# Opening of a decoder-layer kernel: context rows scaled by Pool in the preparation, both input blocks in PSUM, one ring bank beside the scans, merged norm statistics

## What is computed

```python
x = layernorm(x + mamba(x))                 # state of 512 channels x 16, scanned over 512 steps
x = layernorm(x + cross_attention(ctx, x))  # 16 heads of 64; keys and values from 1601 + 512 rows
x = layernorm(x + experts(x))               # 8 experts, 2 chosen, 2 shared

# in mamba, for each channel d and state n
h = exp(dt * A) * h + dt * B * xs           # over time
y = sum_n(h * C) + xs * D                   # then y * silu(z) @ W_out
# in cross_attention
xn = layer_norm(ctx, g1, b1); ln = layer_norm(x, g2, b2)
q = ln @ Wq; k, v = concat([xn, ln]) @ Wkv; softmax(q k / 8) v @ Wout
```

## Time and profile before

| | us |
|---|---|
| median of 3 runs | 3148.29 (3147.78 to 3148.49) |
| the profiled execution | 3144.86 |
| its span | 3143.1 |
| preparation | 0 to 151.05 |
| scans and gate | 151.05 to 289.70 |
| bridge | 289.70 to 342.23 |
| attention and experts | 342.23 to 3143.1 |

### The profile page before, as it was taken

How to read it: one execution, slowest core, us unless ns; L and a number is a source line. 1 busy time by engine, 2 the same in 40 slices (tenths; PEclk the granted TensorE clock), 3 DMA queues, 4 the chain that set the end, 5 groups by cost and what they waited for, 6 DMA issues and landing times. The chain is left out here.

```text
span 3143.1 us, 33934 instructions
## 1 busy us (share of the span) xinstructions
PE 2954.3 (94%) x11590; PEld 1850.7 (59%) x11590; DVE 1973.0 (63%) x3403; ACT 1343.6 (43%) x2309; POOL 1070.3 (34%) x838
## 2 busy tenths in 40 slices
PE   7576899999999999999999999999999999899996
PEld 3233566656665656565656566666656565676666
DVE  5897677775658777666777776665555554452225
ACT  4642454454455454536454544354343434211121
POOL 3196466662006676600376664000000000102213
PEclk9788899999999999999999999999999999899998
DMA  5341221121121111211221212101010100411112
GB/s 218 150 163 68 74 71 58 34 65 55 38 68 58 35 58 35 71 35 38 75 58 35 71 50 63 38 15 40 19 38 15 38 15 14 168 57 53 51 44 69
DMA packets 71679, 189.84 MB, mean 60 GB/s; under 512 B 8420, under 2 KB 39272, under 8 KB 63448
## 3 DMA queue, kind: packets, MB, share of 16 engines
q1 hardware_dynamic: 67096, 172.08, 18.0%
q0 software_dynamic: 3984, 15.60, 1.5%
q10 hardware_dynamic: 432, 0.01, 0.0%
HBM read 124.59 MB, written 28.44 MB: 49 GB/s over the span
## 5 line engine op out<-in xcount | busy, mean ns | idle before, releaser
L987 ACT ACTIVATE a_carry<-a_st 128x512 f32<-128x512 f32 (+1 forms) x1088 | 649.1, 597 | 1126.7 <-PE a_st L1368 1118.7
L1380 PE MATMUL a_o<-a_carry,a_vals 128*65 128x512 f32 (+1 forms) x2176 | 1113.7, 593 | 0.0
L1145 DVE TENSOR_REDUCE a_maxes<-a_mx 128x1 f32<-128x512 f32 x1024 | 683.0, 686 | 220.0 <-PE a_mx L1296 213.3
L1368 PE MATMUL a_st<-a_q,a_kone 65*128 65x512 f32 (+1 forms) x1088 | 431.5, 397 | 0.0
L884 POOL TENSOR_TENSOR a_shared<-a_shared,a_bc 128x512 f32<-128x512 f32 x192 | 251.5, 1310 | 384.9 <-DVE a_shared L1083 384.9
L1380 PEld LDWEIGHTS a_o<-a_carry,a_vals 128*65 128x65 f32 (+1 forms) x2176 | 284.1, 137 | 103.5 <-issue 1.8
L1367 PE MATMUL a_st<-a_q,a_keven 128*128 128x512 f32 (+1 forms) x544 | 325.9, 599 | 0.7 <-issue 0.7
L855 POOL TENSOR_TENSOR a_erstd<-a_emv,a_half 128x4 f32<-128x4 f32 x8 | 8.1, 1014 | 906.9 <-DVE a_emv L1171 906.9
L1367 PE MATMUL a_st<-a_q,a_kodd 128*128 128x512 f32 (+1 forms) x544 | 314.9, 579 | 0.0
L1296 PE MATMUL a_mx<-a_kodd,a_q 128*128 128x512 f32 x512 | 298.4, 599 | 7.2 <-DVE a_maxes L1145 6.1
L1083 DVE TENSOR_TENSOR_SCAN a_shared<-a_shared 128x512 f32<-128x512 f32 x192 | 288.6, 1505 | 12.7 <-POOL a_shared L873 11.6
(11 more groups left out here) (251 smaller groups left out, 4404.9 us busy)
## 6 DMA issues: line engine op xcount, KB each, us to landing
a_bc<-m_kept_bc SPq DMA_DIRECT2D x48, 512.0 KB, 3.7
a_wt<-a_w_split SPq DMA_DIRECT2D x15, 1536.0 KB, 9.5
a_kone<-a_keven SPq DMA_DIRECT2D x32, 528.5 KB, 4.5
a_kone<-a_kodd SPq DMA_DIRECT2D x32, 528.5 KB, 4.2
e_wall<-in_w_t_dram SPq DMA_DIRECT2D x27, 512.0 KB, 9.6
a_early<-m_kept_bc SPq DMA_DIRECT2D x16, 512.0 KB, 3.7
a_w_split<-a_wt POOLq DMA_DIRECT2D x4, 1536.0 KB, 5.5
a_shared<-in_ctx_dram SPq DMA_DIRECT2D x4, 1536.0 KB
```

What stands on the lines that cost most here:

```text
L987: nc.scalar.activation(p_of(s % 4)[0:r], st[0:r, s % 2], ACT.Exp, scale=SCALE).then_inc(exp_done, 1)
L1145: nc.vector.reduce_max(maxes[:, c, t:t + 1], mx[:, i % 2], AX_X).then_inc(mx_max, 1)
L1368: nc.tensor.matmul(st[0:r, s % 2], k_one[g % 2][0:DH + 1, kt * P:kt * P + r], qm[of(g)][0:DH + 1, :], start=False, stop=True).then_inc(st_ ...
L1380: nc.tensor.matmul(ps_o[0:DH + 1, g % 2], vals[0:r, kt * HG + j, :], p_of(s % 4)[0:r], start=(kt == 0), stop=(kt == KT - 1)).then_inc(pv_d ...
```

## The change

- **Preparation.** The context statistics move to the first tap of the last batch's convolution, their sums to behind `clip_dt` of the batch before. Pool then scales all 13 context tiles (`tensor_scalar`) in the preparation. The B and C rows of states 0 and 1 are fetched there (`fetched`), and ScalarE ends with a one-column exponential.
- **Scans.** dt*xs of both channel blocks of a pair is copied to PSUM (`dtu_bank`, two banks), and VectorE makes 40 of the 64 inputs (`BY_DVE`), Pool 24. The third decay buffer takes a ring bank, so the context items share ring bank 0. Context blocks stay in that bank: ScalarE applies the gammas in place, the high part is a step of its own ("h"), the low part reads PSUM. ScalarE copies the values. xs*D enters the sums by a matmul, and `gate_first` only multiplies.
- **Bridge.** Per tile of 128 rows: statistics, then one power for both norms ("g": the second norm's factor follows from the same variance), and one scaling for the attention input ("n"); the first norm's scaling ("j") moves beside head 0. The queries are made per block ("q"). Row scores of head 0 use four banks and start before keys 3 and 4. Rows of ones and of `wo` are set by Pool ("1").

```diff
+            for t in range(CTX_T):
+                r = CL if t == CTX_T - 1 else P
+                nc.gpsimd.tensor_scalar(rows[0:r, t], rows[0:r, t], mv[0:r, t, 0:1], rstd[0:r, t:t + 1], ALU.subtract, ALU.mult)
...
+            nc.scalar.activation(cb[:, 0:1], cb[:, 0:1], ACT.Exp)
...
+                    if j == 0 and i == B - 1:
+                        context_stats(c)
...
-                if i == B:
+                if i == B - 1:
                     context_sums()
...
+                if b == B - 1:
+                    sp.wait_ge(bc_kept, 32 * B)
+                    for n, (place_of, loaded) in enumerate(fetched):
+                        sp.dma_start(place_of.rearrange("p i s -> p (i s)"), kept_bc[b, n].partition_broadcast(P)
+                                     ).then_inc(loaded, 16)
...
+BY_DVE = [u for u in range(NU) if u % 2 == 0 or u % 8 == 3]
...
+    room = {"T": 13, "V": 10, "K": 13}
+    at, all_room = 0, sum(room[what[0]] for what in early)
+    for what in early:
+        step = at * (NU - 2) // all_room
+        at += room[what[0]]
+        later = {"PE": 0, "ACT": 1 if what[0] == "T" else 2, "DVE": 3}[engine]
+        steps[step + later].append(what)
+        if what[0] == "T":
+            steps[step + later + (engine == "ACT")].append(("h",) + what[1:])
+            steps[step + later].append(("U",) + what[1:])
...
-        decay_first, dtu_bank = [mx[:, 0], mx[:, 1], ps_o[:, 1]], ps_o[:, 0]
+        decay_first, dtu_bank = [mx[:, 0], mx[:, 1], ring[:, 1]], [ps_o[:, 0], ps_o[:, 1]]
...
+            def mx_bank(g, i):
+
+                return (st if g == 0 and i % 4 >= 2 else mx)[:, i % 2]
...
             copy_keys(0)
+            sp.wait_ge(ones_set, 2)
+            load_wo(0)
...
+                if c < N_CTX:
+                    made = turned_first(what)
+                    for k in range(KD):
+                        a = nc.scalar.activation(made[:, k], made[:, k], ACT.Identity, bias=gb[:, 1, k:k + 1], scale=gb[:, 0, k:k + 1])
...
+                step(nc.vector.bn_stats(end_stats[:, t], x1_rows(b, t)))
+                step(nc.vector.bn_aggr(end_mv[:, t], end_stats[:, t]))
+                nc.vector.tensor_scalar(both_var[:, t, 0:1], end_mv[:, t, 1:2], EPS, None, ALU.add)
+                nc.vector.tensor_scalar(both_var[:, t, 1:2], end_mv[:, t, 1:2], 1.0 + EPS, EPS * EPS, ALU.mult,
+                                        ALU.add).then_inc(var_ready, 1)
...
-                    s = nc.vector.tensor_tensor(y[:, c], sums(c), y[:, c], ALU.add)
-                s.then_inc(sums_out, 1)
-                dve.wait_ge(sums_out, q + 1)
-                for c in (2 * q, 2 * q + 1):
-                    nc.vector.tensor_tensor(y[:, c], y[:, c], gate[:, c], ALU.mult).then_inc(gated, 1)
+                    nc.vector.tensor_tensor(y[:, c], sums(c), gate[:, c], ALU.mult).then_inc(gated, 1)
...
+            def queries(i):
+
+                t, n, r, col = PREP[i]
+                pe.wait_ge(turned_low, i + 1)
...
+                if n == 0:
+                    nc.tensor.matmul(sums(c), ident[:], y[:, c], start=True, stop=False)
```

More of the change, by code:

```diff
@@ L189, in _ @@
             sp.wait_ge(w_stored, 16 * NG)
+            for place_of, loaded in fetched:
+                sp.wait_ge(loaded, 16)
         @block.gpsimd
@@ L494, in beside @@
             at[6 + t].append(("O", g - 1, t))
+    else:
+        for t in range(TT):
+            at[4 + t].append(("j", 0, t))
     if following and h == 12:
@@ L569, with ring_banks @@
 AT = {x: i for i, x in enumerate(x for x in MADE if x[0] in "QKVOTP")}
+def ring_banks():
+    bank, rank, seen, others = {}, {}, [0, 0], 0
+    for what in AT:
+        if what not in BEFORE:
+            k = others % 2
+            others += 1
+        elif what[0] == "P":
+            k = 1 - what[2] % 2
+        else:
+            k = 1 if what[0] == "T" and what[2] >= N_CTX or what[0] == "K" and what[2] >= 3 else 0
+        bank[what], rank[what] = k, seen[k]
+        seen[k] += 1
+    return bank, rank
+BANK, RANK = ring_banks()
 HIGH = {x: i for i, x in enumerate(x for x in MADE if x[0] in "QK")}
-POW = {x: i for i, x in enumerate(x for x in MADE if x[0] in "EGL" or x[0] == "A" and x[2] == 1)}
+POW = {x: i for i, x in enumerate(x for x in MADE if x[0] in "EGLg" or x[0] == "A" and x[2] == 1)}
 def attention(nc, ctx_rows, g1, b1, g2, b2, wq, wkv, wo, x1):
@@ L598, in attention @@
         half = sb("a_half", [P, NT])
+        halves = shared[:, CTX_T * DM:].rearrange("p (h i s) -> p h i s", h=2, i=2)
+        first_loaded = [sem(f"a_first_loaded{i}") for i in range(4)]
         prepare(nc, ctx_rows, (g1, b1, g2, b2), wq, wkv, w_dram,
-                (carry, y, bc_gate, rows, wt, ident, a_neg, gb, stats, mv, rstd, half))
+                (carry, y, bc_gate, rows, wt, ident, a_neg, gb, stats, mv, rstd, half,
+                 [(halves[:, i], first_loaded[i]) for i in range(2)]))
         st = ctx.enter_context(nc.psum_tensor("a_st", [P, 2, 512], F32))
@@ L901, in _ @@
                     make_rstd(what)
+                elif what[0] == "1":
+                    set_ones()
             for g in range(NH):
@@ L976, in make @@
                     turn(what)
+                elif what[0] == "h":
+                    turned_rows_high(what)
+                elif what[0] == "V" and what in BEFORE:
+                    values(what)
                 elif what[0] == "M":
@@ L1181, in make @@
                 kind = what[0]
+                if kind == "V" and what in BEFORE:
+                    return
                 if kind in "QKV":
@@ L1281, in project @@
                 mm.then_inc(ring_full, 1)
+            def queries(i):
+                t, n, r, col = PREP[i]
+                pe.wait_ge(turned_low, i + 1)
+                if i == N_CTX:
+                    wait_bank(("Q", 0, 0))
+                return product(ring[:, bank(("Q", 0, 0)), col - LC:col - LC + n * r],
+                               *[lambda k, w=w: w[:, k, 0:P] for w in (wqh, wql)],
+                               *[lambda k, w=w: w[:, k, col:col + n * r] for w in (kvh, kvl)])
             def row_scores(g, i):
-                if i == 0:
+                if i == 0 and g == 0:
+                    pe.wait_ge(q_first, 1)
+                elif i == 0:
                     wait_evicted(pe, ("Q", g // 2, 0))
@@ L1343, in make @@
                     project(what)
+                elif kind == "q":
+                    queries(what[2])
                 elif kind == "C":
```

212 lines of the change are left out of this document (136 added, 76 removed).

## The result

The changed kernel takes 3113.35 us in the median (3112.40 to 3116.32, four runs), the kernel before 3148.03 (3145.89 to 3148.49, four runs of the same chip): a ratio of 0.9894, 95% interval 0.9882 to 0.9906. The forecast was 3120.1 us in 3108 to 3134. The profiled execution of after took 3116.32 us for a span of 3114.6. The two spans differ by 28.5 us, where the sum said 28.2; the medians differ by 34.7, because before's profiled execution (3144.86) lay under its median and after's was the longest of its four. So the sum was nearly exact for the pair of traces that it was made on, and in the medians the change brought 6 us more. The same kernel measured again gave 31.7 (3115.94 beside 3147.65), so a few of these microseconds are not settled by one set of runs.

The account below looks back on a forecast made before the run. VectorE was taken to bound the scans, Pool close behind; the bridge was a chain with no engine full. 2.3 - 16.4 - 1.3 - 15.1 + 2.3 = -28.2; 3144.9 - 28.2 + 3.4 = 3120.1 us, range 3108 to 3134.

Parts of the forecast that it names:

- Preparation, +2.3: Stage before the scans: 2.3 us longer, mainly VectorE slowed beside Pool's scalings and convolution taps; bounds 0 and +6.
- The worst bound's 1.3 per piece: Preparation: at worst each of Pool's 13 row scalings takes 1.3 us, so they are done by 135.
- the rival that priced them at 2.67: Preparation: 13 Pool scalings take 35 us, to 153, and VectorE pays 3.8; kernel at 3126 us, chance 0.03.
- The added 1.1 for the sums: Preparation: the statistics' sums (0.96 + 0.17) stand in VectorE's full queue of the batch before, adding 1.1 us.
- Scans, -16.4: Scans beside context projections: end at 269.4 us against 285.8, by an earlier start and faster pace; bounds -22 and -10.
- level, Pool ahead by nothing: Scans: VectorE's 105 us and Pool's 106.3 are level, so neither hides the other's stops.
- the 6 named: Scans: sign of a right forecast, Pool's waits below 6 us.
- 4 us of stops: Scans: 1.0 us at the mid gate and 3 for key and value blocks ahead of state sums, together 4.
- One bank: Rival, scans: all 16 context items go through bank 0, holding it 61.5 us; 3181 in full, 3150 at half; chance 0.06.
- Gate, -1.3: Between last sum and output projection: two additions of 0.65 us leave the chain, 1.3 us shorter.
- Bridge, -15.1: Output projection to first attention scores: shorter norm, turning and row maxima bring the scores at 327.1 us against 342.2.
- Loads, +2.3: Start of attention: batch 1's loads land late, ScalarE waits, TensorE loses 1.6 us plus 0.7 at first scan; bounds 0 and 6.

Follow-up runs that it names:

- the edit: Changed kernel with ScalarE scaling context blocks into SBUF, where high and low parts read them: 3123.91 us.
- each single undo: Changed kernel with one edit undone: products shared 32 and 32, 3120.34 us; low parts from SBUF, 3123.91; context rows scaled by VectorE in the scans, 3122.70.

## Why the prediction was right, point by point

- **Preparation, +2.3.** The pair of traces says +1.9; the change's own part is 1.0, the rest is variation upstream. Right in range, for partly wrong reasons. (VectorE's gaps at the taps of before are two of 1.2 us and one of 2.4, not three and one; the statistics fitted even so.) The price of Pool's scalings was the miss: forecast 0.6 each and 8 us, "done by about 127". Measured they take 23.9 us in all and end at 142.8 (one line's instructions: ns min/median/max, first and last start):

```profile
L230 POOL TENSOR_SCALAR a_shared<-a_shared,a_mv,a_rstd x13: 1214/1224/3146, 118.9 to 141.5; 128x256 f32<-128x256 f32 x12, 65x256 f32<-65x256 f32 x1
```

  The worst bound's 1.3 per piece held for seven of them, not for the first five, at 2.58 to 3.15: the first of these ran beside four taps of 128x512, the others beside VectorE's four operations of 128x2048; the rival that priced them at 2.67 came nearer on Pool, and still lost nothing, since 10 us of cover were left. What they cost VectorE was forecast as 1.5 and 0.7 and is 1.0. The added 1.1 for the sums did not show.
- **Scans, -16.4.** In the pair, the last product ends 15.4 us earlier, 17.2 without the preparation's 1.9. Landmarks: first scan 154.4 (forecast 152.3 + 2.3), third C product 161.1 (159.1 + 2.3), from there to the end 109.4 us (110.3). The low parts at 0.68 were right, and the edit shows what the wrong answer would have cost: not "some 3" but 8.4 (7.6 outside the mid gate). The step "level, Pool ahead by nothing" held: each single undo cost 4 to 9 us. Pool waited 7.9 us in all, over the 6 named. Behind the third product, where the sum had put 4 us of stops, it stood idle 4.1 (the row below: 109.4 us, 105.3 busy in 85 operations). That this fits is partly luck: 1.6 of it is the clock at the mid gate, for which the sum had no term, so the stops that it did name came to about 2.5.

```profile
161.07:270.45 109.38, 84.52 (x242) 35.78 (x240) 100.21 (x112) 54.99 (x91) 105.29 (x85) 0.98 0.46 155
```

- **One bank.** TensorE never held up the scans for it: in the waits of the scans it stands before a context item only once, for the identity copy. Nothing of the 61 us showed.
- **Gate, -1.3.** Measured -1.3.
- **Bridge, -15.1.** Measured -17.0. The chain came out as worked: last scaling 2.7 behind the projection (2.9), row scores 9.9 (9.9), joined maximum 26.8 (26.9). Power took 0.79, not 0.5, and VectorE waited 0.59 for the last one. What the sum lacked is the projection itself, 7.17 instead of 8.59 us, at clock 1.00 instead of 0.83: 1.4. All this is read from the rows; no run undoes the merged statistics and power or the queries per block, so what each of them brought is not shown.
- **Loads, +2.3.** The term that was mis-sized: the last stretch is 5.2 longer, the first head 4.4. ScalarE's wait (5.6, forecast 4.6) costs TensorE up to 2.6, near the forecast 2.3. What the sum lacked in the head is 1.3 at the four scalings and about 0.5 by the longer time at half speed; the remaining 0.8 of the stretch lie behind the first head, where the kernels vary by more. The prediction had put the four VectorE operations at nothing, "beside an engine that is busy 61% there": an average over 2801 us does not say that the engine has room in the one head where they stand. Errors of -1.9 in the bridge and +2.9 here cancelled, and so did smaller ones in preparation (-0.4) and scans (-0.8): that the pair of traces came within 0.3 us of the sum is luck. The bound of 6 held the loads.

The Trainium skill (GPSIMD Engine Reference, Specifications) says that Pool and VectorE share SBUF interfaces and contend when VectorE has two SBUF inputs. The low part at 676 ns with its PSUM operand and at 2253 ns without agrees, and so do the SBUF ones at 0.68 and 0.69 us with no Pool instruction beside them. The 2253 ns are a larger average than the 1550 of before.

## What to carry to other kernels

When two engines are level, an undo of one edit overstates it: add the work on each engine, take the longer, and test by undoing all together. When a stage is shortened, look at what its end also releases, above all loads that had slack only because the stage was slow; issue them by their own dependencies. The four banks' 2.5 us in the bridge came back, but for 0.4 to 0.8, in the first head. And operations that are moved to an engine with idle time on average should be looked for at the place where they land.

## What the runs showed that I had not expected

- TensorE's clock couples a short stop to the stages after it: builds with identical scans took 113.2, 114.8 and 116.0 us, by the clock at the mid gate, the last state sums took 3.8 or 5.5 us up to the projection, and the bridge 33.5 or 35.5, in kernels that differ nowhere near.
- Idle matmuls in the bridge gave back 1.8 us of attention; at the end of the scans they cost as much, by standing in front of the last sum.
- On Pool a subtract and multiply of 128x256 with two per-partition scalars takes 1.22 us, twice its cast of 128x512 at 0.61. The first five of 13 took 2.58 to 3.15, four of them beside VectorE's operations of 128x2048.
- One VectorE subtraction of 128x512 has cost 0.68, 1.13, 1.55 and 2.25 us on average, by where its operand lies and whether Pool works meanwhile.
